# Zeroing the slot tables of the first mixture from another queue and at another time

## The reference

```
edge_index = jnp.stack([src, dst])
x = x + L0_gnn(layernorm(x))   # two GATv2 layers (8 heads x 96, then 1 x 768), elu, norms
x = x + L0_ffn(layernorm(x))   # 8 experts 768 -> 3072 -> 768, gelu, the best 2 of 8 per token
x = x + L1_gnn(...)  + L1_ffn(...)
x = x + L2_gnn(...)  + L2_ffn(...)
x = x + L3_gnn(...)  + L3_ffn(...)
```

```
fs = x @ Ws + bs ; fd = x @ Wd + bd                      # 625 x 768
e = leaky_relu(fs[src] + fd[dst], 0.2)                   # 20000 x 768
logits = einsum('ehd,hd->eh', e, attn)                   # 20000 x 8
alpha = softmax of the logits over the edges of one dst
out = segment_sum(alpha * fs[src], dst) ; elu(out)
```

```
top_p, top_i = top_k(softmax(x @ router_w + router_b), 2)
out = sum over the two chosen experts of weight * (gelu(x @ w1[e] + b1[e]) @ w2[e] + b2[e])
```

## Time and profile before

| what | value |
|---|---|
| median of 3 runs | 4110.46 us (4107.86 to 4110.98) |
| the profiled execution | 4104.76 us, span 4103.0 us |
| busy in the span | PE 60%, DVE 53%, POOL 28%, ACT 19% |
| edges 0: first scatter issue of the 4th tile to the last landing | 145.0 to 879.7 us |
| read of the logit table, then attend 0 | 880.1 to 893.6, then to 973.4 us |
| ELU and layer norm 1 | 973.5 to 1002.0 us |
| linear layers of table layer 1 | 1016 to 1096 us |
| edges 1 | from 1101.7 us, 157 scatters from 1121.7 to 1820.5 us |
| bytes of the 25 zero writes | 25 x 768 KB = 19.7 MB, of 54.3 MB written in all |

### The profile page before, as it was taken

The page is one execution under the profiler, slowest core; times in us unless marked ns, Lnnn a source line. Parts: engine busy times, 40 slices in busy tenths (PEclk is TensorE's granted clock), DMA queues, the critical chain, the costliest instruction groups (busy, mean ns, idle before and its releaser), DMA issues.

```text
span 4103.0 us, 37498 instructions
## 1 busy us (share of the span) xinstructions
PE 2477.2 (60%) x13152; PEld 2028.0 (49%) x13153; DVE 2179.4 (53%) x3944; ACT 769.6 (19%) x1107; POOL 1132.9 (28%) x987
## 2 busy tenths in 40 slices
PE   8445555556600000015599888888588487886899
PEld 4333343345300000003599888888275244475799
DVE  3666677767444444434575455545474524567332
ACT  0000000024000000001364334433072111044110
POOL 0667677730277777750100000000100000000000
PEclk9666655667855555556799999999788687998799
DMA  8666666653365666640675555554300001100111
GB/s 261 198 206 212 213 178 178 172 136 115 99 174 173 176 177 178 179 116 1 196 265 194 171 177 177 179 170 148 114 1 12 10 27 36 58 12 24 70 70 42
DMA packets 117558, 543.01 MB, mean 132 GB/s; under 512 B 31195, under 2 KB 31451, under 8 KB 112220
## 3 DMA queue, kind: packets, MB, share of 16 engines
q0 software_dynamic: 65920, 264.29, 22.1%
q1 hardware_dynamic: 50088, 262.32, 19.0%
q10 hardware_dynamic: 1386, 14.06, 1.1%
HBM read 486.31 MB, written 54.26 MB: 132 GB/s over the span
## 4 chain that ended last, share of the span: by engine, by line
PE 43%; issue 31%; POOL 9%; DMA 8%; DVE 8%; ACT 1%; SPq 0%; POOLq 0%; DVEq 0%; ACTq 0%
PE PS L780 18%; PE PS L642 7%; PE PS L873 6%; DMA logits<-lgr,key 6%; PE PS L697 4%; POOL logits L549 3%; POOL WB L538 3%; POOL WB L541 2%; PE PS L683 1%; PE PS L750 1%; PE PS L854 1%; PE PS L740 1%; DVE stats L1181 1%; PE PS L626 1%; DVE W L1343 1%
## 5 line engine op out<-in xcount | busy, mean ns | idle before, releaser
L611 PE MATMUL PS<-O 128*125 128x512 bf16 (+9 forms) x1727 | 404.9, 410 | 355.5 <-DVE O L1206 344.3
L683 PE MATMUL PS<-ident,W 125*125 125x125 f32 x650 | 113.7, 313 | 811.7 <-issue 737.8
L1254 DVE TENSOR_TENSOR WB<-WB 128x776 f32<-128x776 f32 x276 | 267.4, 969 | 561.9 <-DMA WB<-dst_rows,idx 558.4
L611 PEld LDWEIGHTS PS<-O 128*125 128x125 bf16 x1727 | 275.3, 200 | 485.2 <-DVE O L1206 404.5
L683 PEld LDWEIGHTS PS<-ident,W 125*125 125x125 f32 x650 | 96.1, 215 | 827.0 <-issue 771.9
L780 PE MATMUL PS<-urowsT,w1s 128*128 128x192 f32 (+2 forms) x3492 | 430.4, 283 | 73.2 <-issue 65.6
L549 POOL DMA_INDIRECT logits<-lgr,key x314 | 416.3, 1326 | 210.9 <-DMA logits<-lgr,key 118.8
L780 PEld LDWEIGHTS PS<-urowsT,w1s 128*128 128x128 f32 x3492 | 428.4, 199 | 75.5 <-issue 71.1
L538 POOL DMA_INDIRECT WB<-src_rows,idx x314 | 321.2, 1023 | 293.8 <-DMA dst_rows<-O 198.7
L642 PE MATMUL PS<-WB,XT 128*125 128x384 f32 (+1 forms) x1120 | 377.5, 500 | 13.8 <-DMA WB<-in_L_gnn_Wos 12.6
L780 PE MATMUL PS<-w2s,hid 128*128 128x384 f32 x2016 | 369.0, 336 | 5.3 <-issue 5.3
(11 more groups left out here) (224 smaller groups left out, 3186.8 us busy)
## 6 DMA issues: line engine op xcount, KB each, us to landing
XN<-in_L_ffn_w SPq DMA_DIRECT2D x98, 769.0 KB, 4.4
PB<-in_L_ffn_w SPq DMA_DIRECT2D x97, 768.0 KB, 5.0
logits<-NEG ACTq DMA_DIRECT2D x9, 1367.2 KB
WB<-logits SPq DMA_DIRECT2D x5, 2187.5 KB
slot_rows<-NEG SPq DMA_DIRECT2D x13, 768.0 KB
slot_outs<-NEG SPq DMA_DIRECT2D x12, 768.0 KB
C<-in_L_ffn_expert_w SPq DMA_DIRECT2D x8, 1152.0 KB, 5.5
NEG<-in_L_ffn_expert_w SPq DMA_DIRECT2D x8, 1152.0 KB, 6.5
```

Of the source, the lines that this page charges most:

```text
L611: mm = pe.matmul(PSz[0:R, a:b], oh[:, slot, 1, c * R:(c + 1) * R], oh[:, slot, 0, a - c * N:b - c * N], start=(first and fresh), stop=last ...
L683: tr = pe.transpose(PSz[0:R, 1024 * (1 + s % 2) + b * P:1024 * (1 + s % 2) + b * P + R], src[:, b * R:(b + 1) * R], ident[0:R, 0:R])
L1254: dve.tensor_tensor(gs[u], gs[u], gd[u], ALU.add).then_inc(s_z, 1)
```

## The change

The 25 zero writes leave SP's queue and edges 0. DVE clears a piece of `WB` that the logit tiles don't use (columns 10752 to 12287, called `blank`) between `mask_start` and `mask_end`. POOL, behind `edges(0)` and ahead of `rsqrt(1)`, waits for that and for `s_lm` at 8, which is the end of the fronts of node tile 0, and then issues the 25 writes one behind the other. DVE no longer waits for them. Since `linear_weights(3)` overwrites `blank`, SP waits for all 25 between the two weight loads of layer 1. The bytes and the number of writes stay as they were.

```diff
+        blank = WB[:, 10752:12288]
...
+        s_blank = sem("blank_rows_ready")
...
                 params(g)
                 if g:
                     sp.wait_ge(s_out, units_before(g, ("table",)))
-                    for side in range(2):
-                        linear_weights(2 * g + side)
+                    linear_weights(2)
+                    sp.wait_ge(s_zslots, SLOTS0)
+                    linear_weights(3)
...
-                if g == 0:
-
-
-                    zeros = NEG[:, :, :].rearrange("p t n -> p (t n)")
-                    zeroed = 0
-                    for table, units in ((slot_rows, NU + 1), (slot_outs, NU)):
-                        flat = table.rearrange("(a p b) d -> a p (b d)", a=units, p=P)
-                        for a in range(units):
-                            zeroed += 1
-                            sp.wait_ge(s_sc, 16 * 3 * zeroed)
-                            sp.dma_start(flat[a], zeros[:, 0:SU * D]).then_inc(s_zslots, 16)
                 sp.wait_ge(s_sc, 16 * ET * (g + 1))
...
             rsqrt(0)
             edges(0)
+            pool.wait_ge(s_blank, 1)
+            pool.wait_ge(s_lm, 8)
+            for table, units in ((slot_rows, NU + 1), (slot_outs, NU)):
+                flat = table.rearrange("(a p b) d -> a p (b d)", a=units, p=P)
+                for a in range(units):
+                    pool.dma_start(flat[a], blank).then_inc(s_zslots, 16)
             rsqrt(1)
...
                     dve.wait_ge(s_zeroed, LOGITS0)
-                    dve.wait_ge(s_zslots, SLOTS0)
                     mask_start()
+                    dve.memset(blank, 0.0).then_inc(s_blank, 1)
                     mask_end(0)
```

## The result

| | before | after |
|---|---|---|
| first comparison, median | 4109.16 us (4101.91 to 4110.98, 4 runs) | 4063.89 us (4060.64 to 4066.92, 4 runs) |
| ratio, 95% interval | | 0.9893 [0.9876, 0.9910] |
| profiled execution | 4104.76 us | 4065.49 us (span 4063.1) |
| the same two again, five rounds | 4103.67 us (4093.45 to 4111.30, 23 runs) | 4066.86 us (4062.96 to 4073.33, 6 runs) |
| ratio, 95% interval | | 0.9914 [0.9897, 0.9930] |

Faster, as forecast, but by 45 us in the first comparison where 34 were forecast, and 2 us under the low end of the range. By the profiled executions it is 39 us, by the second comparison's ratio 35 (29 to 42).

The account below looks back on a forecast made before the run. Edges 0 was taken as bound by late-landing scatters during zero writes, then by POOL's issue work. Terms -35.0 + 0.1 + 0.0 + 0.5 + 0.4 = -34.0 us gave 4070.8 profiled, 4076.5 median; range 4066 to 4092.

Parts of the forecast that it names:

- The cadence of edges 0: First 72 scatter intervals of edges 0 run like the later 74 without zero writes: 35.0 us gained, bounds 0 and 88.
- The correction for slow early tiles: Edges 0: first tiles may be a little slower by themselves, as in edges 1, taking 3.0 us off 36.4.
- Rivals 1 and 4: Edges 0: 1, it gets faster than its second half, 4050 us, 5%; 4, first 72 tiles slow by themselves, 4111, 4%.
- The memset: DVE's added memset in the tail of edges 0 may hold a scatter longer: 0.1 us cost, bounds 0 and 1.3.
- From the profiled run to the median: Whole kernel: median of runs taken as 5.7 us above the profiled execution, turning 4070.8 into 4076.5 us.
- The collision in attend 0: Zero writes beside reads of logit tiles 2 to 4, engines taking turns: 0.5 us cost, bounds 0 and 19.
- Rival 2: Attend 0: engines share queues by time, not turns; each read 9.95 us more, net -15, 4095 us; 7%.
- POOL's queue: Attend 0: POOL issues 25 writes at 1.02 us each, 25.5 us, free long before the inverse root; zero cost.
- work beside DVE: Attend 0: POOL's descriptor writing may stretch DVE's instructions; 0.4 us cost, at most 1.5.
- Rival 3: Inverse root after attend 0 stuck behind POOL's DMAs: mild 4089 us, 4%; hard 4221 us, 4%.
- Cover of the writes: Attend 0 to second-layer loads: 63.6 us of room for 47 us of writes; zero cost, upper bound 2 us.

Follow-up runs that it names:

- the two repeats: No edit: the kernel before and the changed kernel each run and profiled again beside the kernel before; ratios 1.0007 and 0.9914.
- the direct test: Changed kernel without POOL's wait for eight fronts, so the 25 writes lie beside the first logit table reads; 4070.87 us, ratio 0.9922 to the kernel before.

## Why the prediction was right or wrong

**The cadence of edges 0: right.** The term was 35.0 us, from 33.4 to 36.4. The trace pair gives 36.0, the two repeats 369.2 - 328.9 = 40.3 (its kernel before had a cadence of 5.13). With 12 writes, or with 25 over twice as many tiles, the price was 1.6 to 1.7 us each, near the 1.46 of the 36.4 us over 25 writes. The correction for slow early tiles was not needed: the first stretch is as fast as the second (4.575 and 4.588). Rivals 1 and 4 are out.

**The memset: the step that failed.** "So 0.1 us, bounds 0 and 1.3." Scatter 149 to the last became 4.2 us shorter in the first trace pair, and scatter 149 to the first front 3.3 us. In the five traces without the memset and with no wait ahead of the masks it is 27.8 to 29.5 us, in the seven with the memset 24.1 to 26.4. The working saw that a scatter beside DVE's long instructions is held, and reckoned the memset as one more of these. It isn't one: a scatter ends inside it (833.20 in the trace shown), so it parts two instructions that hold POOL and lets a scatter through. The reading that the long add "moves hardly at all" was right (4.73 us behind the first mask instruction before, 5.07 after), but one scatter more now passes ahead of it, so that the last starts 7.8 us behind that instruction in place of 10.9. The bounds excluded a gain without a reason. The size is 3 to 4 us.

**From the profiled run to the median: the larger term that failed.** "The median of the runs is 5.7 us above it." The forecast of 4076.5 us was 12.6 above the measured 4063.89. Of these, 5.3 us lie in the profiled execution, 4065.49 in place of 4070.8: its parts are the memset (3.4 us by the first front), the cadence (1.0), and small gains and losses in stages that the edit does not touch. The other 7.3 are this step: the changed kernel's median lay 1.6 us under its profiled run, not 5.7 above. The 5.7 were three runs' chance: 92 runs of the kernel before, over all comparisons, lie between 4088 and 4121 us, with a median of 4105.4, and the ten of the changed kernel have 4065.8, 39.6 less, as much as the profiled executions give. The second comparison gives 35 us (29 to 42), which holds the forecast. What the first comparison's 45 us have above the 39 of the profiled executions has no place in any trace. That it was the draw of the runs is the likeliest reading, but a single comparison of four and four runs can't be taken apart afterwards.

**The collision in attend 0: right, its price by luck.** 0.5 us was taken; the fronts of tiles 2 to 4 lost nothing. Rival 2 (sharing by time) is out by the direct test: 1.75 us on a read, not 8 to 10. The queues do take turns, but the 1.8 us reckoned for the turns of a read were 0.7 at most, and the 1.75 match a late start (1.76) that the prediction did not have.

**POOL's queue: right, and cheaper than reckoned.** 0.53 us a write in place of 0.72 + 0.3, none held. The 0.4 us for work beside DVE did not come either: DVE was busy 66.75 us in place of 66.78. Rival 3 is out even for 50 writes: its inverse root never waited. Descriptor writing beside the fused instruction of DVE was not slowed (0.531 us is the least and the median), so the Trainium skill's rule on the lock ("SBUF — State Buffer", section "SBUF: two separate sides") bears on the tail of edges 0 and not on attend 0. Whether that lies in the plain writes or in the fused instruction no run parts.

**Cover of the writes: right.** They ended about 947 us, before the loads at 964.5 to 967.9; the experiment with twice as many shows that less than a second helping fits.

## What to carry to other kernels

Where one engine issues small dependent DMAs one after the other, a large transfer beside them costs the chain most of its own engine time (here 1.5 to 1.7 of 1.88 us a write), though the engines look only two thirds busy; move it to a stage in which the DMA engines have time left, and compute the room in engine time, not in queues. When an instruction is put between others, ask what it parts and not only what it adds, and leave the bound open on the side of gain. Keep DVE's long instructions between SBUF buffers away from a chain of POOL-issued DMAs: a wait that holds DVE back costs nothing where a table read covers it.

## What the runs showed of the hardware

- DVE instructions do not all hold POOL's indirect DMAs alike. Beside the copy of 125x3125 out of PSUM (3.41 us) scatters took their 0.97 us, and one ended within the memset of SBUF; beside the tensor_scalar and the two-input add between SBUF buffers they took up to 3.51 and 3.49. A held scatter ended 0.83 to 0.84 us after the instruction, or 0.12 us after the second of two back to back (870.33 in the kernel before). A gap of 0.03 us was enough: the scatter of 835.08 ended at 836.44, inside the add that had begun at 835.64.
- POOL took 50 writes of 768 KB, 39 MB, in 27 us with none waiting, though none landed in under 12.6 us; on SP's queue every issue from the ninth on was held, most often for 1.58 us.
- A queue with packets of 20,000 bytes and one with packets of 6144 moved 129 and 125 of them side by side. A read of 2.5 MB issued behind such writes moved its first row after 2.34 us in place of 0.58 and landed after 15.51 us in place of 13.76.
